# The scatter stage of a fused state-space and expert layer: W2 on 32x32 stationary tiles, block transposes on VectorE, bias by a one-hot product

## The reference: what is computed

```python
grouped = x.reshape(b, s // g, g, d)                       # g = 32 tokens
logits = jnp.einsum('bntd,des->bntes', grouped, Wc) + bc
logits = logits + tie
perm = (logits == jnp.max(logits, axis=-3, keepdims=True)).astype(x.dtype)
permuted = jnp.einsum('bntd,bntes->bnesd', grouped, perm)
inner = jax.nn.relu(jnp.einsum('bnesd,esdf->bnesf', permuted, W1) + b1)
result_permuted = jnp.einsum('bnesf,esdf->bnesd', inner, W2) + b2
result = jnp.einsum('bnesd,bntes->bntd', result_permuted, perm)
```

## Time and profile before

| what | value |
|---|---|
| time, median of 3 runs | 3000.07 us (2998.5 to 3001.02) |
| profiled execution, span | 3002.6 us (its own run time is not listed apart) |
| PE busy | 2871.7 us, 96% |
| DVE, ACT, POOL busy | 2053.3, 1713.5, 1430.4 us |
| data moved | 328.99 MB |

### The profile page before, as it was taken

How to read it: one execution, slowest core, us unless ns; L and a number is a source line. 1 busy time by engine, 2 the same in 40 slices (tenths; PEclk the granted TensorE clock), 3 DMA queues, 4 the chain that set the end, 5 groups by cost and what they waited for, 6 DMA issues and landing times.

```text
span 3002.6 us, 134681 instructions
## 1 busy us (share of the span) xinstructions
PE 2871.7 (96%) x59324; PEld 2453.1 (82%) x59324; DVE 2053.3 (68%) x2982; ACT 1713.5 (57%) x3751; POOL 1430.4 (48%) x2287
## 2 busy tenths in 40 slices
PE   8999999999999999999999999996787879999999
...
DMA packets 372550, 328.99 MB, mean 110 GB/s; under 512 B 62960, under 2 KB 284656, under 8 KB 371328
## 3 DMA queue, kind: packets, MB, share of 16 engines
...
## 4 chain that ended last, share of the span: by engine, by line
PE 90%; DVE 4%; issue 3%; DMA 1%; SPq 1%; POOL 1%; ACT 0%; ACTq 0%; DVEq 0%; POOLq 0%
PE a_proj L992 40%; PE a_mix L992 11%; PE s_rt L1748 8%; PE g_pick_ps L1462 5%; PE a_scan L1106 5%; PE s_w_ps L1716 5%; PE s_rt L1761 4%; DVE g_picked L1393 3%; PE a_scan L1083 3%; PE a_scan L1070 2%; PE g_acc_ps L1486 2%; PE a_mix L1058 2%; PE a_misc L1050 1%; PE a_misc L1124 1%; DMA part_dram<-res 1%
## 5 line engine op out<-in xcount | busy, mean ns | idle before, releaser
L992 PE MATMUL a_proj<-wdh,xTh 128*128 128x512 f32 x1024 | 420.9, 411 | 5.0 <-issue 3.1
L1679 ACT COPY s_res<-s_rt 128x512 f32<-128x512 f32 x512 | 262.9, 601 | 245.8 <-PE s_rt L1748 245.8
L992 PE MATMUL a_proj<-wdh,xTl 128*128 128x512 f32 x1024 | 402.0, 393 | 0.0
L992 PE MATMUL a_proj<-wdl,xTh 128*128 128x512 f32 x1024 | 400.0, 391 | 1.5 <-issue 1.5
L824 DVE COPY_PREDICATED scan_in<-mask,a_scan 64x512 f32<-64x512 uint32 x512 | 382.3, 747 | 16.0
L1693 DVE TENSOR_TENSOR s_resT<-s_w_ps,s_b 128x1024 f32<-128x1024 f32 (+1 forms) x252 | 293.1, 1205 | 136.4 <-PE s_w_ps L1716 136.4
L465 POOL TENSOR_TENSOR dx<-xs,d_row 64x512 f32<-64x512 f32 x256 | 330.3, 1290 | 15.1
L640 ACT ACTIVATE scan_in<-CT,hsel 64x128 f32<-64x128 f32 x1024 | 326.0, 388 | 4.9
L473 POOL TENSOR_TENSOR yv<-yt,dx 128x512 f32<-128x512 f32 x128 | 188.6, 1473 | 292.8 <-DVE yt L864 292.8
L604 ACT ACTIVATE raw<-a_proj,rs 128x272 f32<-128x272 f32 x128 | 62.5, 488 | 427.6 <-PE a_proj L992 427.6
L1393 DVE COPY g_picked<-g_pick_ps 128x1024 f32<-128x1024 f32 x128 | 156.7, 1224 | 216.3 <-PE g_pick_ps L1462 216.3
...
## 6 DMA issues: line engine op xcount, KB each, us to landing
x<-in_x_dram SPq DMA_DIRECT2D x128, 256.0 KB, 2.7
xn_dram<-xn SPq DMA_DIRECT2D x128, 256.0 KB, 2.4
part_dram<-res SPq DMA_DIRECT2D x128, 256.0 KB, 2.5
g_xn<-xn_dram SPq DMA_DIRECT2D x512, 64.0 KB, 2.3
s_w<-in_w_dram SPq DMA_DIRECT2D x128, 256.0 KB, 4.1
s_part<-part_dram SPq DMA_DIRECT2D x128, 256.0 KB, 3.9
out_dram<-s_out SPq DMA_DIRECT2D x128, 256.0 KB, 3.0
xr<-in_xT_dram SPq DMA_DIRECT2D x126, 256.0 KB, 2.8
```

Source lines behind the costliest of these rows:

```text
L992: last = nc.tensor.matmul(out, lhs[a], rhs[c], start=(k == 0 and n == 0), stop=(k == nk - 1 and n == 2))
L1679: nc.scalar.copy(res[:, n % 4, :, :], rt_bank[:, n % 3, :, :]).then_inc(res_cp, 1)
```

## The change

The scatter stage is written anew, with small adaptations before it.

- The sets become 16 of 32 groups (`SG` = 32), and the features are cut in 2 halves of 256 columns (`NH`, `DH`) instead of 4 quarters; the halves are now the outer loop. There are 32 steps of 4 units (`QB`), again 128 units; `LAG` is 8.
- W2: `inner` becomes the stationary operand (32 rows of an expert x 32 groups) and W2 the moving one (256 columns). 32 products per unit go to 16 places of 32x32. The result has groups on partitions. W2 of a half stays in SBUF for 16 steps; `inner` and `permT` are loaded once per step.
- ACT copies the result from PSUM into `stage` (`evict`, two copies of 128x1024 per unit). DVE turns it in blocks of 32x32 into `turned` (four `transpose` per step, 128x2048 each, both sides with a step of 256 float32 numbers between elements), so that experts are on partitions.
- The bias is no longer added behind W2. `b2` is split into a rounded part and its rest (`round_b2`, `rest_b2`), and each output tile gets perm x b2 by two float32r products of 256 columns before the one-hot product of `turned` is added in PSUM.
- DVE adds the partials from PSUM, two token tiles x 256 columns at a time; there are three buffers of partials. Output and partials are written in pieces of 256 columns.
- The gather stage clamps and adds `b1` in halves of 32 groups, and stores `inner` in that layout; all eight last stores stand together, ahead of the first loads of partials.

The diff, cut to its core:

```diff
@@ -53,11 +53,10 @@
 GB = 64
 GT = GB * GRP // P
 NGB = TOK // (GB * GRP)
-SG = 128
+SG = 32
 NSET = TOK // (SG * GRP)
-STL = SG * GRP // P
-NW = 8
-QW = NQ // NW
+NH = 2
+DH = D // NH
...
+    def inner_view(b, i, h):
+        return inner[b % 2][:, h, 2 * QW * i:2 * QW * (i + 1), :].rearrange("p q (r t) -> p q r t", r=GPT)
+    def acc_view(i, h):
+        groups = acc_bank[:, halves(i), :, :].rearrange("p j q (r h t) -> p (j q) r h t", r=GPT, h=GB // SG)
+        return groups[:, :, :, h, :]
...
-        quads = slice(PQ * piece, PQ * piece + PQ)
+        x, h = divmod(piece, 2)
+        quads = slice(2 * PQ * x, 2 * PQ * (x + 1))
         eng.wait_ge(biased, 2 * b + 1 + 2 * piece // PIECES)
-        eng.dma_start(inner_dram[b][:, quads, :], inner[b % 2][:, quads, :]).then_inc(inner_out[b % 2], 16)
+        eng.dma_start(inner_dram[2 * b + h][:, quads, :], inner[b % 2][:, h, quads, :]).then_inc(inner_out[b % 2], 16)
...
+                for h in range(GB // SG):
+                    half = inner[b % 2][:, h, quads, :]
+                    last = nc.gpsimd.tensor_tensor(half, half, b1[:, quads].unsqueeze(2).to_broadcast([P, 2 * QW, SG]), ALU.add)
+                last.then_inc(biased, 1)
...
+        scatter["round_b2"](act)
         for u in range(4):
-            scatter["add_b2_last"](act, u)
+            scatter["evict"](act, u)
...
+            lower = b1neg[:, 2 * QW * i:2 * QW * (i + 1)].unsqueeze(2).unsqueeze(3)
+            for h in range(GB // SG):
+                last = nc.vector.tensor_tensor(inner_view(b, i, h), acc_view(i, h),
+                                               lower.to_broadcast([P, 2 * QW, GPT, SG // GPT]), ALU.max)
+            last.then_inc(acc_cp, 1)
...
+        scatter["rest_b2"](dve)
...
+        bank = ctx.enter_context(nc.psum_tensor("s_ps", [P, 8, 2, DH], F32))
...
+    QB = 4
+    UNITS = NH * NSET * QB
+    STEPS = NH * NSET
+    LAG = 2 * QB
+    CT = SG * GRP
+    DT = DH // 4
+    NPART, NOUT, NINNER = 3, 3, 3
+    w2 = sb("w2", [P, QB, 8, DH], at=AT_W1)
+    stage = [sb(f"stage{i}", [P, EX // 4, DH], at=a) for i, a in enumerate((AT_XNT, AT_W1 + 32768))]
+    turned = [sb(f"turned{i}", [P, SG, DH], at=AT_PICKED + 32768 * i) for i in range(2)]
+    inner = [sb(f"inner{i}", [P, NQ, SG], at=a) for i, a in enumerate((AT_PERM1, AT_PERM0, AT_XN3 + 12288))]
+    perm = [sb(f"perm{i}", [P, CT], F32R, at=AT_XN3 + 4096 * i) for i in range(2)]
+    permT = [sb(f"permT{i}", [P, CT], BF16, at=AT_XN3 + 8192 + 2048 * i) for i in range(2)]
+    b2 = [sb(f"b2{n}", [EX, D], F32R, at=AT_TOP + 2048 * i) for i, n in enumerate("hl")]
+    b2_raw = sb("b2_raw", [EX, D], at=AT_TOP + 4096)
     ones = sb("ones", [P, 1], at=AT_TOP + 6144)
-    part = [sb(f"part{i}", [P, UT, P]) for i in range(NPART)]
-    out = [sb(f"out{i}", [P, UT, P], at=AT_TOP + 2048 * i) for i in range(NOUT)]
-    small_in = sem("small_in")
-    w2_in = [sem(f"w2_in{w}") for w in range(NW)]
-    inner_in = [sem(f"inner_in{w}") for w in range(NW)]
+    part = [sb(f"part{i}", [P, 2, DH]) for i in range(NPART)]
+    out = [sb(f"out{i}", [P, 2, DH]) for i in range(NOUT)]
...
+    part_dram = keep["part"].rearrange("k p (v t) c -> k v p t c", t=2)
+    out_dram = io["out"].rearrange("(v t p) (k c) -> k v p t c", p=P, t=2, k=NH)
...
+    def pair(u, h):
+        first = h if u < 4 else (2 * u + h) % 3
+        return slice(2 * first, 2 * first + 2)
+    def load_w2(sync, k, i):
+        sync.dma_start(w2[:, i, :, :], io["w2"][k, i]).then_inc(w2_in[i], 16)
+    def load_inner(sync, m):
+        s = m % NSET
+        if m < NSET:
+            sync.wait_ge(gat["inner_out"][s // 2 % 2], gat["inner_count"] * (s // 4 + 1))
+        sync.dma_start(inner[m % NINNER][:], keep["inner"][s]).then_inc(inner_in[m % NINNER], 16)
+    def load_perm(sync, m):
+        sync.dma_start(permT[m % 2][:], perm_dram[m % NSET]).then_inc(perm_in[m % 2], 16)
...
+    def load_first(sync, w):
+        if w == 3:
+            sync.wait_ge(gat["perm_ps"], NGB)
+            sync.dma_start(b2_raw[:], io["b2"]).then_inc(b2_in, 16)
+            for m in range(2):
+                load_inner(sync, m)
+        if w in (8, 12):
             for i in range(2):
+                load_w2(sync, 0, w // 2 - 4 + i)
+        if w == 15:
+            for m in range(2):
+                load_perm(sync, m)
+            load_inner(sync, 2)
...
+        for u in range(UNITS + LAG + 1):
+            m, i = divmod(u, QB)
+            if u < UNITS and (m == NSET - 1 or i == QB - 1):
+                sync.wait_ge(w2_ps, u + 1)
+            if m == NSET - 1:
+                load_w2(sync, 1, i)
+            if i == QB - 1 and m + NINNER < STEPS:
+                load_inner(sync, m + NINNER)
+            v = u - LAG - 1
+            if v >= 0:
+                store(v)
+                if v + NPART < UNITS:
+                    load_part(v + NPART)
+                m, x = divmod(v, QB)
+                if x == 1 and m + 3 < STEPS:
+                    sync.wait_ge(perm_ready, m + 2)
+                    load_perm(sync, m + 3)
+            elif u == LAG - 1:
+                sync.wait_ge(perm_ready, 1)
+                load_perm(sync, 2)
...
+        def spread_perm(m):
+            pool.wait_ge(perm_in[m % 2], 16 * (m // 2 + 1))
+            wait(pool, out_ps, QB * (m - 1))
+            nc.gpsimd.tensor_tensor(perm[m % 2][:], permT[m % 2][:], ones[:].to_broadcast([P, CT]), ALU.mult).then_inc(perm_ready, 1)
+        pool.wait_ge(att["res_cp"], 2 * NST)
         nc.gpsimd.memset(ones[:], 1.0).then_inc(zeroed, 1)
         pool.wait_ge(zeroed, 1)
-        for n in range(NC * NSET):
-            s, c = divmod(n, NC)
-            pool.wait_ge(perm_in[n % 2], 16 * (n // 2 + 1))
-            if s > 0:
-                pool.wait_ge(out_ps, STL * (KD * s - 1) + (c + 1) * STL // NC)
-            nc.gpsimd.tensor_tensor(perm[:, c * CT:(c + 1) * CT], permT[n % 2][:], ones[:].to_broadcast([P, CT]),
-                                    ALU.mult).then_inc(perm_ready, 1)
-    def add_b2_last(act, u):
-        m, w = divmod(u, NW)
-        if u == 0:
-            act.wait_ge(small_in, 32)
+        for m in range(STEPS):
+            spread_perm(m)
...
+    def round_b2(act):
+        for i in range(2):
+            act.wait_ge(att["res_out"][i], 16 * NST)
+        act.wait_ge(b2_in, 16)
+        nc.scalar.copy(b2[0][:], b2_raw[:]).then_inc(b2_hi, 1)
+    def rest_b2(dve):
+        dve.wait_ge(b2_hi, 1)
+        nc.vector.tensor_tensor(b2[1][:], b2_raw[:], b2[0][:].bitcast(F32), ALU.subtract).then_inc(b2_lo, 1)
+    def evict(act, u):
+        m, i = divmod(u, QB)
         act.wait_ge(w2_ps, u + 1)
-        for q in range(QW):
-            e = EW * w + 4 * q + 3
-            for j in range(2):
-                last = nc.scalar.activation(resT[m % 2][j][:, :, e], w2_place(u)[:, 3, q, j * GB:(j + 1) * GB],
-                                            ACT.Identity, bias=b2[:, m % KD, e:e + 1])
-        last.then_inc(res_last, 1)
+        wait(act, turn_cp, 4 * (m - 1))
+        places = stage[m % 2][:, 8 * i:8 * i + 8, :].rearrange("p (j r) d -> p r j d", r=4)
+        for h in range(2):
+            nc.scalar.copy(places[:, 2 * h:2 * h + 2, :, :], bank[:, pair(u, h), :, :]).then_inc(w2_cp, 1)
...
+        for u in range(4, UNITS):
+            evict(act, u)
...
+        def add_part(v):
+            dve.wait_ge(out_ps, v + 1)
             dve.wait_ge(part_in[v % NPART], 16 * (v // NPART + 1))
             wait(dve, out_done[v % NOUT], 16 * (v // NOUT))
-            nc.vector.tensor_tensor(out[v % NOUT][:], out_bank.rearrange("p (t d) -> p t d", d=P),
-                                    part[v % NPART][:], ALU.add).then_inc(out_cp, 1)
+            nc.vector.tensor_tensor(out[v % NOUT][:], bank[:, 6 + v % 2, :, :], part[v % NPART][:], ALU.add).then_inc(out_add, 1)
+        for m in range(STEPS):
+            dve.wait_ge(w2_cp, 2 * QB * (m + 1))
+            wait(dve, out_ps, QB * (m - 1))
+            for y in range(4):
+                cols = slice(DT * y, DT * y + DT)
+                nc.vector.transpose(turned[m % 2][:, :, cols].rearrange("p n d -> p d n"),
+                                    stage[m % 2][:, :, cols].rearrange("p e d -> p d e")).then_inc(turn_cp, 1)
+                if m > 0:
+                    add_part(QB * (m - 1) + y)
+        for v in range(UNITS - QB, UNITS):
+            add_part(v)
+    def apply_w2(pe, u):
+        m, i = divmod(u, QB)
+        k, s = divmod(m, NSET)
+        if s == 0:
+            pe.wait_ge(w2_in[i], 16 * (k + 1))
+        if i == 0:
+            pe.wait_ge(inner_in[m % NINNER], 16 * (m // NINNER + 1))
+        if u == 4:
+            pe.wait_ge(gat["acc_cp"], 2 * NGB)
+        wait(pe, w2_cp, 2 * u if u < 4 else 2 * u - 1)
+        for j in range(2):
+            for c in range(4):
+                for r in range(4):
+                    rows_ = slice(ES * r, ES * r + ES)
+                    dst = bank[32 * c:32 * c + 32, pair(u, r // 2), :, :][:, r % 2, j, :]
```

(31 more changed lines are left out.)

203 lines of the change are left out of this document (18 added, 185 removed).

## The result

| | before | after |
|---|---|---|
| median of 4 runs each, us | 3000.1 (2998.5 to 3001.02) | 3105.95 (3102.61 to 3106.94) |
| ratio, 95% interval | | 1.0344 [1.0332, 1.0356] |
| profiled span, us | 3002.6 | 3104.8 |
| one steady unit of the scatter stage, us | 4.03 (TensorE) | 4.75 (VectorE) |
| moved by DMA, MB | 328.99 | 316.37 |

The change makes the kernel 3.4% slower. The forecast was 2859 us, in a range of 2822 to 2960, so the result lies outside it, on the other side. It is the first rival, written at 3125.

The account below looks back on a forecast made before the run. TensorE bounded the kernel before; DVE would bound the scatter stage at 2.90 us per unit. Handover, steady units, tail and small charges summed to a 2862 us span, 140.7 less than 3002.6; forecast 3000.07 - 140.7 = 2859 us, range 2822 to 2960.

Parts of the forecast that it names:

- first rival: Scatter stage: strided transposes cost double, up to 4.45 us each, unit 4.97 us, total 3125 us, slower by 4%; chance 0.19.
- the size of the transpose: Scatter stage, DVE: one 128x2048 block transpose takes 2.29 us, between bounds of 1.15 and 4.45.
- 1.05 slope: DVE's time per element, 1.05 ns, with a fixed part of 143 ns, used to size the 2048-element transpose.
- PE's unit: Scatter stage: TensorE work per unit falls from 4.03 to 2.7 us, below DVE's 2.90.
- second rival: Scatter stage, W2 products: small tiles run no wider than 8, PE unit 3.5 to 4.1 us, total 2926 to 2998; chance 0.12.
- one-hot group: Scatter stage, PE: 8 one-hot products of 256 columns instead of 16 of 128, still 1.01 us per unit.
- handover: Gather to scatter stage: paced about as now, last clamp ends near 2481, first step's transposes take 9 us, to 2490.
- additions: Scatter stage, DVE: one 128x512 addition from PSUM per unit, 0.68 us.
- ACT 2.02 a unit: Scatter stage: ACT's two PSUM copies take 2.02 us per unit, under DVE's 2.90.
- loss in the gather stage: Gather stage: 32 clamps of 0.68 us replace 16 of 1.21, adding 2.4 us on DVE, charged as 2.
- late partials: Scatter stage: partials load three units (8.7 us) ahead against 3.9 to land, costed at nothing; if late, each stalls DVE.
- slowing by POOL: Scatter stage: POOL's permutation expansion beside DVE operations costs nothing, 61 us at worst.

Follow-up runs that it names:

- e3: The changed kernel with its block transposes reading and writing contiguous numbers (result altered): 2923.71 us, beside 3002.76 for the kernel before.
- f2: The changed kernel with both transpose buffers laid out features outermost, ACT writing pairs of neighbours and stepping through PSUM: ratio 0.9998 to the kernel before.
- e1: The changed kernel with its block transposes reading a contiguous slab, the write still strided (result altered): 3047.63 us.
- e2: The changed kernel with its block transposes writing contiguously, the read still strided (result altered): 3050.53 us.
- g1: The changed kernel, computation whole, with each 16-byte line of both transpose buffers holding 2 features of 2 neighbours: 2924.27 us, ratio 0.9726 to the kernel before.
- g2: g1 without ACT's wait for the last stores of inner ahead of its fifth evacuation: 2917.11 us, ratio 0.9702 to the kernel before.

## Why the prediction was wrong

- **The step that failed: the size of the transpose.** I bounded it by 1.15 and 4.45 us and took 2.29, "since the only transpose row and four other DVE rows lie on the 1.05 slope". It measured 4.33, and the steady units that rest on it account for 230 of the 243 us by which the span exceeded the sum. The upper end was nearly exact. The slope was right too (2.30 us, e3), for contiguous numbers; what I carried over without a row was that the slope holds for single numbers 1 KB apart in SBUF. The four rows read PSUM, and the one transpose row has a short contiguous side of 32 numbers.
- **The argument that chose wrongly.** I set the PSUM rows (2 KB steps at full rate) against the Trainium skill's rule on SBUF's lines (SBUF — State Buffer, section Specifications), and let them decide for SBUF. They are right about PSUM: f2's ACT copies read it at such steps in 1066 ns. They did not carry over to SBUF, where e1 and e2 show 3.85 and 3.93 us for one strided side; this trace agrees with the rule. The prediction even named the gap, that in SBUF these lines write runs of 3 to 16 numbers and never single ones. With no row for the case and a rule of the Trainium skill against it, the two ends deserved nearer to equal chances than 0.60 and 0.19.
- **The first rival came true with its own numbers**: unit 4.97 written, 4.75 measured; 3127 us of span written, 3104.8 measured. Its point of decision, about 3.3 us a transpose, fits the eight kernels that edit L1691 alone: those with 3.85 and over were slower than before, those with 2.37 and under faster, and none lay between.
- **PE's unit: 3.10, not 2.7.** W2 took 1.43 us for the 1.10 forecast, and the bias with its changes of shape 0.67 for 0.58. The second rival (narrow tiles, W2 of 1.9 to 2.48) didn't come true. In the timeline W2's 64 weight loads take 1.01 us, then 0.41 pass until the next shape begins; the one-hot group shows 0.59 and the same 0.41. So the 32x32 group looks held by its number of instructions, 16 ns each. That is read off the rows; no run varied it, so it is not shown. In the change this cost nothing, DVE being the bound; with contiguous transposes (e3, 2923.71 us) it makes the unit 3.10 for my 2.90, 25 us in 124 units.
- **The handover: 2504.0 for 2493.** Timeline of after:

```profile
2485.28 16.56 DVE L1691 STREAM_TRANSPOSE s_turned<-s_stage 128x2048 f32<-128x2048 f32 x4
...
2491.60 1.93 ACT L1671 COPY s_stage<-s_ps 128x1024 f32<-128x1024 f32 x2 [7.75 <-DMA inner_dram<-g_inner]
...
2504.00 4.37 DVE L1691 STREAM_TRANSPOSE s_turned<-s_stage 128x2048 f32<-128x2048 f32 x1 [2.16 <-ACT s_stage L1671]
```

  Of these 11 us, 7.6 are the first four transposes again (16.56 us for the 9 written), 2.2 the wait for ACT; the transposes begin at 2485.28, 1.3 us later than 2481 and the 3 us allowed for. I had seen the wait for the stores in SP's queue only, not in ACT's; with short transposes it costs more, as g1 and g2 show.
- **Right:** additions 0.68 (measured 0.68), one-hot group 1.01 (1.00), ACT 2.02 a unit (1.93 for two), no visible loss in the gather stage (its last copies from PSUM start on DVE at 2465.03, before at 2465.32), no late partials that DVE waited for in the change, no slowing by POOL (transposes in 2560:2900 average 4.34 us beside its expansion of the permutation and 4.35 away from it).
- **Forecast against the repaired kernel:** g1 has everything the forecast assumed of the change, and takes 2924, not 2859; its span is 2924.1 for the 2861.9 of the sum, 62 us more. PE's unit explains 25 us of it and the handover 12 (2505.42 for 2493). The rest, 25 us, is that g1's units average 320 / 97 = 3.30 us in 2560:2880 and not 3.10 (0.20 x 124). 4.1% of the chain there (13 us) is "issue", the longest gaps 1.6 to 1.8 us, and DVE waits 5.8 us in all for late partials. What makes these gaps stays open. Some cost more than their length, because TensorE's granted clock falls behind them:

```profile
2601.83 0.65 PE L1714 MATMUL s_ps<-s_w,s_inner 32*32 32x256 f32 x12 [1.78 <-issue]
...
2604.94 2.00 PE L1714 MATMUL s_ps<-s_w,s_inner 32*32 32x256 f32 x64
```

  Behind this gap the clock is 0.70 in 2604:2608, and from start to next start the one-hot group takes 1.86 us instead of 1.00 and W2 1.93 instead of 1.43.
